# New places for the pieces of the attention schedule, with the opening's weight loads, splits and stores placed one by one

## What is computed

```python
x = x + _layernorm(attention(_layernorm(x), w_qkv, b_qkv, w_out, b_out))
x = x + _layernorm(moe(_layernorm(x), router, gate_up, down, sh_gate, sh_up, sh_down, shared_gate))
```

## Time and profile before

| | us |
|---|---|
| median of 3 runs | 1953.87 (1952.63 to 1955.94) |
| the profiled execution | 1956.51, its span 1954.7 |
| PE busy | 1876.6 (96% of the span) |
| DVE, ACT, POOL busy | 1084.2, 842.1, 438.3 |

### The profile page before, as it was taken

One profiled execution on the slowest core, in us unless ns is written; L12 is line 12 of the kernel. 1 busy time (PEld: TensorE's weight loads), 2 busy tenths in 40 slices (PEclk: granted clock), 3 DMA queues, 4 the chain that ended last, 5 costly groups with the idle time before them and its releaser, 6 DMA issues.

```text
span 1954.7 us, 27560 instructions
## 1 busy us (share of the span) xinstructions
PE 1876.6 (96%) x9880; PEld 1529.3 (78%) x9880; DVE 1084.2 (55%) x2590; ACT 842.1 (43%) x1718; POOL 438.3 (22%) x438
## 2 busy tenths in 40 slices
PE   7789999999999998999999999999999999999997
PEld 5566777777777776777777778778999999999875
DVE  4556665454564563464454454353666667666566
ACT  4433443333343233334244233112666666666554
POOL 2301001001001000100100100120355666655322
PEclk9899999999999999999999999999999999999999
DMA  8988557656466447537647456687788989998597
GB/s 309 371 275 301 204 204 275 222 172 231 162 234 238 167 166 258 202 119 261 207 179 253 175 175 237 236 332 258 215 250 261 280 260 262 268 266 249 135 280 198
DMA packets 140869, 456.84 MB, mean 234 GB/s; under 512 B 17200, under 2 KB 17344, under 8 KB 123968
## 3 DMA queue, kind: packets, MB, share of 16 engines
q1 hardware_dynamic: 90720, 251.70, 36.7%
q0 software_dynamic: 49584, 203.33, 33.8%
q10 hardware_dynamic: 432, 0.07, 0.0%
HBM read 332.99 MB, written 122.04 MB: 233 GB/s over the span
## 4 chain that ended last, share of the span: by engine, by line
PE 88%; DVE 5%; DMA 3%; ACT 2%; issue 1%; another core or an unknown queue 0%; SPq 0%; POOL 0%; ACTq 0%; DVEq 0%
PE banks L797 24%; PE banks L799 24%; PE banks L798 24%; PE banks L866 5%; PE banks L880 2%; PE banks L886 2%; PE banks L992 2%; DMA att_w_lo<-att_w_split 1%; PE banks L873 1%; PE banks L830 1%; PE banks L998 1%; DMA out<-x 1%; PE banks L860 1%; DVE fin_stats L1538 0%; PE banks L908 0%
## 5 line engine op out<-in xcount | busy, mean ns | idle before, releaser
L797 PE MATMUL banks<-xT_hi,ffn_gate_up_hi_lo 128*128 128x512 f32 x704 | 288.5, 410 | 9.7 <-DMA xT_lo<-xt_scratch 3.2
L799 PE MATMUL banks<-xT_hi,ffn_gate_up_hi_lo 128*128 128x512 f32 x704 | 276.3, 392 | 0.0
L798 PE MATMUL banks<-xT_lo,ffn_gate_up_hi_lo 128*128 128x512 f32 x704 | 275.4, 391 | 0.0
L1070 ACT COPY q_one_head<-qT 32x128 f32<-32x128 f32 x512 | 150.9, 295 | 121.9 <-PE banks L866 116.8
L797 PE MATMUL banks<-moe_gu_hi,moe_xT_hi 128*128 128x352 f32 x568 | 189.4, 333 | 0.0
L799 PE MATMUL banks<-moe_gu_hi,moe_xT_lo 128*128 128x352 f32 x568 | 183.3, 323 | 0.0
L798 PE MATMUL banks<-moe_gu_lo,moe_xT_hi 128*128 128x352 f32 x568 | 182.6, 321 | 0.0
L797 PEld LDWEIGHTS banks<-xT_hi,ffn_gate_up_hi_lo 128*128 128x128 f32 x704 | 132.9, 189 | 44.3 <-issue 7.0
L683 POOL DMA_INDIRECT ffn_out<-moe_y,moe_x x71 | 124.9, 1760 | 155.4 <-ACT moe_gu_hi L1131 59.8
L798 PEld LDWEIGHTS banks<-xT_lo,ffn_gate_up_hi_lo 128*128 128x128 f32 x704 | 133.0, 189 | 29.2 <-issue 3.6
L799 PEld LDWEIGHTS banks<-xT_hi,ffn_gate_up_hi_lo 128*128 128x128 f32 x704 | 132.5, 188 | 28.8
(11 more groups left out here) (318 smaller groups left out, 4139.8 us busy)
## 6 DMA issues: line engine op xcount, KB each, us to landing
ffn_gate_up_hi_lo<-ffn_gate_up_split SPq DMA_DIRECT2D x66, 1024.0 KB
ffn_down_hi_lo<-ffn_down_split SPq DMA_DIRECT2D x66, 512.0 KB, 4.4
att_w_hi<-att_w_split SPq DMA_DIRECT2D x112, 256.0 KB, 5.3
att_w_lo<-att_w_split SPq DMA_DIRECT2D x112, 256.0 KB, 5.8
x_normed_by_expert<-x_normed POOLq DMA_DIRECT2D x26, 771.0 KB, 15.9
ffn_w_raw<-w_ffn SPq DMA_DIRECT2D x44, 384.0 KB, 6.0
ffn_gate_up_split<-ffn_gate_up_hi_lo SPq DMA_DIRECT2D x11, 1024.0 KB, 4.9
x_in<-x SPq DMA_DIRECT2D x32, 256.0 KB, 5.2
```

The source lines that it names most:

```text
L797: pe.matmul(out_ap, l_hi, r_hi, start=start, stop=False)
L798: pe.matmul(out_ap, l_hi, r_lo, start=False, stop=False)
L799: return pe.matmul(out_ap, l_lo, r_hi, start=False, stop=stop)
L1070: op = act.copy(qz[r, g % 2, j, :], qT[r, g, c * P:(c + 1) * P])
```

## The change

All lists of `PLACES` and `OPENING` get new numbers. In `OPENING`, `W` and `ws`, which had the same places (store right behind split), get places of their own, and so do the raw loads `wa`. Three waits that asked for the last weight split by number (`W 15`, `W 11`, `W 15`) now ask for the latest of all the splits that they need, since the splits may stand in another order. The lists that matter here:

```diff
 PLACES = {
-    "xin": (-26.4, -18.45, -12.88, -12.18,),
-    "N1A": (0.76,),
+    "xin": (-31.04, -27.79, -17.7, -8.51,),
+    "N1A": (-2.17,),
...
-    "wa": (5.53, 5.95, 9.34, 7.63, 9.92, 10.43, 10.08, 11.83, 11.97, 14.59, 17.75, 18.03, 22.85, 22.12, 24.74, 23.59,),
-    "QK": (10.53, 10.62, 11.56, 13.74, 13.91, 14.68, 16.42, 16.92,),
-    "xr": (20.24, 26, 38.27, 43.74,),
+    "wa": (5.54, 5.69, 8.61, 6.59, 12.68, 12.73, 14.51, 13.26, 14.7, 15.26, 17.92, 17.98, 24.06, 23.47, 26.25, 24.91,),
+    "QK": (9.93, 11.07, 11.82, 13.97, 15.46, 15.68, 16.31, 16.61,),
+    "xr": (26.96, 31.35, 44.19, 46.64,),
...
-    "KT": (19.4, 26.64, 34.86, 44.31,),
+    "KT": (19.53, 27.82, 35.02, 45.1,),
...
-    "R1": (58.3,),
+    "R1": (58.66,),
...
 OPENING = {
-    "wa": (0, 0.1, 0.2, 0.3, 0.4, 0.5, 0.6, 0.7, 11, 12, 13, 14, 17, 18, 19, 20,),
-    "W": (3.07, 3.17, 7.17, 8.17, 10.88, 11.32, 13.32, 14.32, 15.32, 16.32, 17.32, 18.17, 23.02, 23.17, 23.32, 23.47,),
-    "ws": (3.07, 3.17, 7.17, 8.17, 10.88, 11.32, 13.32, 14.32, 15.32, 16.32, 17.32, 18.17, 23.02, 23.17, 23.32, 23.47,),
+    "wa": (8.41, 12.32, 6.49, 10.01, 11.2, 12.75, 16.81, 8.29, 25.84, 23.51, 25.11, 23.15, 20.05, 26.72, 27.42, 35.72,),
+    "W": (5.63, 3.57, 6.65, 8.17, 8.94, 12.96, 14.84, 14.88, 18.47, 15.5, 19.12, 18.71, 24.28, 22.33, 23.48, 24.75,),
+    "ws": (18.01, 16.15, 25.86, 18.01, 21.89, 27.13, 27.7, 28.25, 34.39, 39.09, 37.41, 40.09, 40.09, 42.57, 44.16, 47.45,),
...
-                    sp.wait_ge(v_piece, done("V", "W", 0, NW - 1))
+                    sp.wait_ge(v_piece, max(done("V", "W", 0, u) for u in range(NW)))
...
-                        pe.wait_ge(v_piece, done("V", "W", a, 11))
+                        pe.wait_ge(v_piece, max(done("V", "W", a, 8 + k) for k in range(KT)))
...
-                        pe.wait_ge(v_piece, done("V", "W", a, 15))
+                        pe.wait_ge(v_piece, max(done("V", "W", a, 12 + k) for k in range(KT)))
```

More of the change, by code:

```diff
@@ L78 @@
 PLACES = {
-    "xin": (-26.4, -18.45, -12.88, -12.18,),
-    "N1A": (0.76,),
-    "N1B": (1.5,),
-    "N1": (2.9, 3.12, 5.27, 6.92,),
-    "T1": (4.5, 5.23, 6.86, 8.49,),
-    "wa": (5.53, 5.95, 9.34, 7.63, 9.92, 10.43, 10.08, 11.83, 11.97, 14.59, 17.75, 18.03, 22.85, 22.12, 24.74, 23.59,),
-    "QK": (10.53, 10.62, 11.56, 13.74, 13.91, 14.68, 16.42, 16.92,),
-    "xr": (20.24, 26, 38.27, 43.74,),
-    "Z": (15.86, 16.56, 19.94, 22.44, 23.06, 23.79, 27.42, 31.25, 32.46, 33.89, 35.74, 36.2, 41.98, 42.12, 43.83, 46.29,),
@@ L99 @@
-    "T2": (41.94, 42.01, 56.51, 57.66,),
-    "xto": (59.68,),
-    "R1": (58.3,),
[L102 to L110, removed]
+    "xin": (-31.04, -27.79, -17.7, -8.51,),
+    "N1A": (-2.17,),
+    "N1B": (0.25,),
+    "N1": (2.43, 2.81, 3.21, 7.58,),
+    "T1": (4.43, 4.77, 7.23, 8.72,),
+    "wa": (5.54, 5.69, 8.61, 6.59, 12.68, 12.73, 14.51, 13.26, 14.7, 15.26, 17.92, 17.98, 24.06, 23.47, 26.25, 24.91,),
@@ new lines @@
+    "QK": (9.93, 11.07, 11.82, 13.97, 15.46, 15.68, 16.31, 16.61,),
+    "xr": (26.96, 31.35, 44.19, 46.64,),
+    "Z": (14.16, 14.54, 19.42, 21.7, 23.58, 26.27, 26.32, 28.37, 31.86, 32.24, 36.92, 38.57, 41.31, 41.39, 43.65, 46.23,),
+    "KT": (19.53, 27.82, 35.02, 45.1,),
+    "S": (19.43, 20.62, 23.38, 24.58, 27.36, 27.65, 31.02, 31.25, 33.65, 36.07, 39.24, 39.4, 43.28, 43.33, 47.14, 47.67,),
+    "V": (21.48, 22.13, 23.2, 25.1,),
+    "IP": (22.87, 26.02, 29, 32.86, 36.97, 40.56, 46.34, 49.93,),
@@ new lines @@
+    "ST": (26.1, 34.06, 40.86, 50.2,),
+    "OUT": (29.07, 35.13, 44.52, 50.57,),
+    "LO": (36.77, 50.92,),
+    "LN": (38.19, 52.99,),
+    "L": (38.32, 52.76,),
+    "LX": (41.33, 54.35,),
+    "x1o": (39.98, 40.9, 55.19, 59.68,),
+    "T2": (42.14, 42.37, 56.45, 57.67,),
+    "xto": (58.56,),
+    "R1": (58.66,),
+    "R2": (59.86,),
+    "SM1": (59.91,),
+    "SM2": (59.98,),
+    "SM3": (61.75,),
+    "SM4": (61.81,),
+    "CM": (63.09,),
+    "RK": (64.86,),
+    "sc": (66.34,),
+    "PG": (66.59,),
@@ L122 @@
     "T1": (4.47, 5.52, 6.47, 6.59,),
[7 rows of a table removed]
-    "OUT": (29.33, 35.83, 44, 50.42,),
[7 rows of a table added]
+    "OUT": (28.77, 33.45, 46.06, 50.82,),
 }
```

## The result

The changed kernel takes 1969.91 us (median of 4 runs, 1967.12 to 1972.67), the kernel before 1954.69 beside it (4 runs): ratio 1.0081 with an interval of 1.0068 to 1.0094, **15.2 us slower**. The forecast was 1974.2 in a range of 1954 to 1982. The profiled execution took 1972.67 with a span of 1970.9, 16.2 above the span before; the places are compared in these two traces.

The account below looks back on a forecast made before the run. PE, busy 1876.6 of 1954.7 us, was taken as the bound, so only its idle and slow time can move. The terms 2.1 - 5.0 - 8.1 + 31.3 = +20.3 us on the median 1953.87 gave 1974.2, range 1954 to 1982.

Parts of the forecast that it names:

- `wa a,6` behind `wa a,7`: SP's queue, blocks 2 to 7: the load lands late beside POOL's store, PE waits at QK a,6; +31.3 us.
- The clock's share: Behind the late-weight idle at QK 6, PE's clock is granted at its lower level: 1.5 us more per block.
- `KT a,1`: In the blocks, behind `S a,1,0` and `S a,1,1`: PE's 6.0 us bank read-out wait is freed; -5.0 us.
- `xti 3`: Block 5, ahead of `wa 5,4`: the 6.08 us wait at QK 5,5 and its half clock go; -8.1 us.
- The opening up to 116 us: Raw loads, splits and evictions trade places; a microsecond or two on PE is covered by DMA; 0.
- the DMA stretch: Opening, 43 to 116 us: DMA share 1.03 at 369 GB/s covers a microsecond or two of change on PE.
- `ws 0,15`: Opening, behind `xr 0,2` and `xr 0,3`: `wa 1,0` waits for its landing, QK 1,0 at 125.0; +2.1 us.
- rival 1: Blocks: the sixth weight is in time and the gains stand alone; -11.0 us, 1942.9; chance 0.15.
- Rival 2: Blocks: the late-weight wait is short, about 2.3 us, with the clock kept; +2, 1956; chance 0.10.
- Rival 3: Block 5: the gain does not come because `wa 5,4` is late instead; +8 on the forecast, 1982; chance 0.05.

Follow-up runs that it names:

- Experiment 2: The changed kernel with POOL's store `xto a` also waiting for QK a+1,6 on PE, SP's order untouched: 1948.8 us, ratio to before 0.9932.
- experiment 1: The changed kernel with `wa a,6` right behind `wa a,5` in SP's order (blocks 1 to 7): ratio to before 0.9914.
- 4: The kernel before with `wa a,6` behind `wa a,7` on SP (blocks 2 to 7) as its one edit: ratio to before 1.0069.
- experiment 7: The changed kernel, two variants: `ws 0,15` right behind `ws 0,14`, ratio to before 1.0057; `ws 0,2` right behind `ws 0,3`, ratio 1.0052.
- before, `KT a,1` late: The kernel before with `KT a,1` behind `S a,1,0` and `S a,1,1` on PE and DVE (blocks 1 to 7): ratio to before 0.9979.
- after, old weight lists: The changed kernel with the opening's lists `wa`, `W` and `ws` taken from the kernel before: ratio to before 1.0073.
- after, fills released early: The changed kernel with POOL's first two zero fills released by QK 0,6 and QK 0,7 instead of S 0,0,0 and S 0,0,1: ratio to before 1.0087.
- both, combined: The changed kernel with `wa a,6` right behind `wa a,5` and the whole `OPENING` list of the kernel before: ratio to before 0.9960.
- experiment 6: The kernel before with `wa 5,4` behind `xti 3` and `wl 34,0` on SP, in block 5 alone: ratio to before 0.9955.

## Why the prediction was right, and where its sizes were off

**`wa a,6` behind `wa a,7`: +31.3, measured 26.7.** The mechanism is as told: third on SP's queue (second in block 2), beside POOL's store, late at QK 6 in blocks 2 to 7 and nowhere else. Experiment 2 shows that the store makes it late, 1 and 4 that the place in the order does. The waits are 18.1 us for 22.3: in block 4 `wa 4,6` landed 11.7 us behind the end of QK 4,3, where I had 12.3 to 12.5, and the blocks differ more than I allowed, 1.97 in block 7 and 4.60 in block 5. The clock's share was right in sum, 8.4 us of work time for 9.0, and wrong in its reason: I had it only behind idle times over 2.5 us. In this trace the clock is at its lower level behind waits of 1.90 and 1.97 us too; over all traces that have such waits at QK 6 it is so behind 14 of the 20 that are 1.9 to 2.2 us long, and behind all 28 of 3.0 us and more.

**`KT a,1`: -5.0, and `xti 3`: -8.1, in the blocks together -17.9.** Alone on the kernel before they bring 4.1 and 8.8 by the ratios, near the forecast. The stretch of the kernel of experiment 1 is 17.9 us shorter than that of before, 4.8 more than these terms: 14.1 of it is idle time, of which 6.0 at `KT`, 3.2 for weights (6.1 less at QK 5,5, 3 more elsewhere, above all the first OUT), and 3.2 small waits of S and IP (lines 866 and 873) which I had not counted; 3.8 is work time.

**The opening up to 116 us: 0, measured +2.5 to +4.3.** This step failed, and it failed twice. First, `KT 0,0` did not stay in its place: PE ran it at 48.93 instead of 42.48 us. ACT waits 6.8 us at `W 0,6` for the landing of `ws 0,2`, PE behind it 3.4 us; without that wait (experiment 7) `KT 0,0` runs at 46.78, which is a third of the 6.4 us. Second, the DMA stretch did not cover this. PE's S pieces release the zero fills of which the stretch is made: the first fill came 6.5 us later, and the engines moved less. POOL's first start and the windows, before and then after:

```profile
43.22 0.85 POOL L610 DMA_DIRECT2D ffn_out<-x_normed  x1 [25.28 <-PE banks L860]
43.00:60.00 17.00, 14.38 (x74) 10.60 (x74) 7.87 (x14) 4.25 (x12) 5.33 (x7) 1.00 1.02 369
```

```profile
49.75 0.85 POOL L610 DMA_DIRECT2D ffn_out<-x_normed  x1 [35.30 <-PE banks L860]
43.00:60.00 17.00, 15.91 (x65) 11.93 (x65) 7.10 (x13) 5.51 (x14) 3.21 (x5) 0.97 0.86 307
```

`x1o 0,0` landed, and let `xr 0,2` start, at 119.43 instead of 115.10. The kernel before was the earliest of its kind: `xr 0,2` starts at 115.1 to 119.1 in the four traces with the opening of before, and at 119.0 to 121.8 in the five with that of after, 2.5 us later in the mean.

The last link is not what it seems. `x1o 0,0` was started 3.2 us later (98.50, before 95.34), and this has a plain cause: PE's first matmul of `IP 0,2` runs at 91.01, before at 88.17, behind DVE:

```profile
84.35 1.28 DVE L1206 BATCH_NORM_STATS2 pair_stats<-projected 128x6 f32<-128x512 f32 x2
...
87.80 0.69 DVE L1371 TENSOR_TENSOR state_new<-banks,own_block 128x512 f32<-128x512 f32 x1
88.52 1.14 DVE L1374 SCALAR_TENSOR_TENSOR state<-state,state_decay,state_new 128x128 f32<-128x128 f32 x4
89.57 0.69 DVE L1359 TENSOR_TENSOR q_decayed<-qT,decay_q 128x512 f32<-128x512 f32 x1
```

`ST 0,1` now stands behind `OUT 0,1`, so its update of the state (1.8 us) runs behind the norm `LO` that begins at 84.35, and right ahead of what PE waits for; before it was done at 78.17 to 80.0, ahead of `LO`, and the last of these lines began at 86.14. Of the 3.4 us in which it is later 1.8 are this, the rest PE's own lateness. But the landing of `x1o 0,0` does not follow its start. The rows are times in us, the last column is GB/s between 43 and 116 us:

| kernel | first fill | `x1o 0,0` started | `xr 0,2` started | QK 1,0 | GB/s |
|---|---|---|---|---|---|
| before | 43.22 | 95.34 | 115.10 | 122.84 | 369 |
| before, `KT a,1` late | 44.01 | 95.46 | 119.11 | 126.95 | 354 |
| after | 49.75 | 98.50 | 119.43 | 130.08 | 347 |
| after, old weight lists | 44.38 | 99.13 | 119.60 | 127.77 | 344 |
| after, fills released early | 47.23 | 96.05 | 119.53 | 129.96 | 347 |
| both, combined | 44.24 | 100.59 | 117.16 | 130.59 | 356 |

The store that was started last of all landed before four others, and one that was started as in the kernel before landed 4 us later. In these six traces the landing goes with the rate at which the engines have moved bytes up to then. Which of the new places lowers that rate stays open: the late first fill is not all of it, since with the old weight lists the first fill comes at 44.38 and the rate is 344 all the same, and no run moved `ST 0,1` alone.

**`ws 0,15`: +2.1.** The term was 1.4 us earlier up to this store and some 3.6 more behind it. The second part came as told: from the start of `xr 0,2` to QK 1,0 it is 7.2 to 7.8 us in the four traces with the opening of before, 10.1 to 10.8 in the five with that of after, so +2.9 in the mean, and 6.8 with this one store taken out of the way. The first part was lost in the failed step above. A reading was off too, without effect on the sum: the 19.99 us of the earlier trace rows are those of `x1o 0,1`, started at 95.89; `x1o 0,0` was started at 95.34 and took 19.7.

In the sum the prediction's +20.3 was 9.4 us high on the three terms of the blocks (31.3 - 13.1 = 18.2, measured 8.8) and 5.1 low in the opening (2.1, measured 7.2 in this pair of traces and 5.4 in the mean of four and five), so about half of the error in the blocks was hidden by that in the opening: that the total came so near is in part luck. So is the agreement of rival 1: with the sixth weight in time the span is 1943.7, 11.0 under the 1954.7 of before, but this is 17.9 less in the blocks and 6.7 more in the opening, where rival 1 had 13.1 less and 2.1 more, and on one chip the ratio gives 16.8. Rival 2 had waits of 2.3 us with the clock kept; the six waits are 3.0 us in the mean, and the clock fell behind all six in this trace. Rival 3 is excluded by the traces of after and of experiment 6, where no wait for a weight stands at QK 5,4 or QK 5,5.

## What to carry to other kernels

On an in-order queue the load that costs need not be the largest: here 256 KB that PE asks for only some 8 us after they are released came too late six times, because a store on another queue took the engines in between, and moving this one load two places up the queue was worth 27 us in the traces. Where transfers seem to cover an engine's delay, ask what starts them: if it is that engine, the stretch can itself become less full, and then it ends later. Look for this in the rate and in the landing, not in the start of the last transfer: here the start moved by 5 us and the landing did not follow it. Lists of places that were made together don't come apart: half of one and half of the other gave a wait of 11 us where each alone has 5 to 6.

## What the runs showed that was not expected

- The waits for a late weight come in steps: of the 48 at QK 6 in eight traces 20 are 1.9 to 2.2 us, 19 are 3.0 to 3.3, nine are 3.7 to 5.0, and none lies between 2.2 and 3.0. The steps are about the 1.2 to 1.6 us that SP needs for one start beside the store; that this is their cause was not tried.
- The length of a wait does not tell whether the very next matmul is slow: behind 3.2 us it took 0.47 us in block 4 and 0.74 in block 3. But in the 4 us behind each of the six the granted clock was 0.50 to 0.70, behind 1.90 us too, where before the change 2.45 us in the opening had cost nothing. So a wait of 2 us costs its clock in one trace and not in another: at QK 6 of block 2 behind 1.90 us it fell in this trace, and behind 1.93 us in the second trace of the same kernel it stayed whole.
- The same kernel before took 1954.7, 1956.4, 1963.7 and 1964.6 us on the chips of the four comparisons, 0.5% apart, and the changed kernels do not follow in proportion: the difference of two ratios from two chips was 4 to 10 us off that of the spans.
